# Cross-attention and gated FFN on one core: the sums of a group of heads are added up behind the values of the next group's fourth step instead of its third

## The reference, cut to what matters

```
x = x + xattn(layernorm(x), ctx_2048, mask, ...)     # B=2, N=512, C=512, 1024 context rows, 16 heads of 32
x = x + ffn(layernorm(x), ...)                       # hidden size 1408, weights int - 128, scaled

xattn:  q = w8a8_linear(x, wq, bq)                   # rows quantised to -127..127
        k = cond @ wk.T + bk ;  v = cond @ wv.T + bv
        attn = softmax(q k / sqrt(32) + mask)
        return w8a8_linear(attn v, wo, bo)
ffn:    down(silu(gate(x)) * up(x))
```

## Time and profile before

| | us |
|---|---|
| median of 3 runs | 514.65 |
| lowest, highest | 513.08, 515.75 |
| the profiled execution | 512.79 |
| its span | 511.0 |

### The profile page before, as it was taken

How to read it: one execution, slowest core, us unless ns; L and a number is a source line. 1 busy time by engine, 2 the same in 40 slices (tenths; PEclk the granted TensorE clock), 3 DMA queues, 4 the chain that set the end, 5 groups by cost and what they waited for, 6 DMA issues and landing times.

```text
span 511.0 us, 6924 instructions
## 1 busy us (share of the span) xinstructions
PE 470.5 (92%) x2377; PEld 305.8 (60%) x2377; DVE 365.5 (72%) x482; ACT 262.1 (51%) x465; POOL 243.8 (48%) x134
## 2 busy tenths in 40 slices
PE   4999987799798999999999999998979999899996
PEld 3788765577544455454545454433358878788885
DVE  2889756588758878787878978779876468455235
ACT  3678765322166577575756597467624312322220
POOL 3003300901276879788787869796422212223220
PEclk9999997999989999999999999999989999999999
DMA  7898998993288907346180900030034333336412
GB/s 244 284 339 336 356 290 267 247 352 128 83 183 255 209 18 151 77 95 133 50 178 2 207 21 2 1 124 2 1 124 144 125 123 124 123 124 236 156 62 82
DMA packets 44388, 77.40 MB, mean 151 GB/s; under 512 B 5280, under 2 KB 13504, under 8 KB 44352
## 3 DMA queue, kind: packets, MB, share of 16 engines
q1 hardware_dynamic: 44352, 76.94, 51.2%
HBM read 57.95 MB, written 18.87 MB: 150 GB/s over the span
## 4 chain that ended last, share of the span: by engine, by line
PE 61%; DVE 15%; DMA 5%; issue 4%; ACT 2%; SPq 1%; POOL 1%; ACTq 0%; DVEq 0%; POOLq 0%
PE ps L811 8%; PE ps L781 8%; PE ps L833 8%; PE ps L918 8%; PE ps L919 8%; DVE neg_m L1369 5%; DVE p_sum L1518 5%; PE ps L942 4%; PE ps L941 4%; DMA q_lo_d<-kq_lo 3%; PE ps L730 3%; DMA q_st<-q_hi_d 2%; PE ps L741 2%; PE ps L655 2%; PE ps L656 2%
## 5 line engine op out<-in xcount | busy, mean ns | idle before, releaser
L1369 DVE TENSOR_REDUCE neg_m<-ps 128x1 f32<-128x1024 f32 x128 | 150.1, 1217 | 36.2 <-PE ps L781 36.1
L1119 ACT ACTIVATE p_t<-ps 128x512 f32<-128x512 f32 x256 | 137.2, 598 | 47.7 <-PE ps L811 40.6
L1693 POOL TENSOR_TENSOR p_sum<-p_sum,p_t 128x1024 f32<-128x1024 f32 x46 | 109.6, 2394 | 3.2 <-ACT p_t L1119 0.8
L811 PE MATMUL ps<-q_st,k_st 97*128 97x512 f32 x256 | 97.7, 429 | 5.8 <-ACT p_t L1119 5.7
L1693 POOL TENSOR_TENSOR p_sum<-p_t 128x1024 f32<-128x1024 f32 x30 | 72.0, 2404 | 49.9 <-ACT p_t L1119 39.6
L781 PE MATMUL ps<-k_st,q_st 96*128 96x512 f32 x256 | 82.6, 404 | 5.1 <-DVE mask_sb L1467 1.7
L811 PEld LDWEIGHTS ps<-q_st,k_st 97*128 97x128 f32 x256 | 47.7, 189 | 58.1 <-ACT p_t L1119 36.8
L918 PE MATMUL ps<-xt_hi,k_st 128*128 128x512 f32 x176 | 70.6, 401 | 1.4 <-DVE xt_lo L1475 1.4
L919 PE MATMUL ps<-xt_lo,k_st 128*128 128x512 f32 x176 | 69.7, 396 | 0.0
L1641 POOL TENSOR_TENSOR v_st<-v_st,bv_bc 128x512 f32<-128x512 f32 x16 | 20.1, 1281 | 102.7 <-DVE qin L1314 33.9
L833 PE MATMUL ps<-p_t,v_gr 128*32 128x512 f32 x512 | 68.9, 611 | 0.0
(11 more groups left out here) (138 smaller groups left out, 662.1 us busy)
## 6 DMA issues: line engine op xcount, KB each, us to landing
k_st<-k_hi_d SPq DMA_DIRECT2D x16, 512.0 KB, 6.7
mask_sb<-in_mask SPq DMA_DIRECT2D x3, 2048.0 KB, 10.2
w_int<-in_w_gate SPq DMA_DIRECT2D x22, 256.0 KB, 2.8
w_int<-in_w_up SPq DMA_DIRECT2D x22, 256.0 KB, 3.0
w_int<-in_w_down SPq DMA_DIRECT2D x22, 256.0 KB, 3.6
raw<-in_ctx_t SPq DMA_DIRECT2D x16, 256.0 KB, 5.4
k_hi_d<-kq_hi SPq DMA_DIRECT2D x16, 256.0 KB, 4.0
k_lo_d<-kq_lo SPq DMA_DIRECT2D x16, 256.0 KB, 4.6
```

What stands on the lines that cost most here:

```text
L811: mm = pe.matmul(ps[:, bank, :], k_st[g % SLOTS][0:rows, j, P * lc:P * lc + P], q_st[g % SLOTS][0:rows, j, :], start=True, stop=not with_mask)
L1119: act.activation(p_t[:, q % 4, j, :], ps[:, score_bank(lc, j), :], ACT.Exp).then_inc(exp_done, 1)
L1369: dve.tensor_reduce(neg_m[:, g % 2, nt, j:j + 1], ps[:, bank:bank + 2, :], AX_XY, ALU.max, negate=True).then_inc(max_read, 1)
L1693: pool.tensor_tensor(total, former, p_t[:, q % 4, hs, :], ALU.add).then_inc(added_pool, 1)
```

## The change

One constant, `SUM_LC`, from 2 to 3:

```diff
         SET = 4
-        SUM_LC = 2
+        SUM_LC = 3
         TURN_LC = 4
         HOLD = 1
```

## The result

Over 15 runs of each, the kernel before took 513.58 us (median; 512.42 to 516.38) and the changed one 516.00 us (514.88 to 518.75). The ratio is 1.0052, with a 95% interval from 1.0034 to 1.0071: 1.7 to 3.6 us slower, 2.7 us in the middle. The forecast of +0.8 us (515.4) had the sign, and the time lies in its range, but the step was some three times as large. That 515.4 is only 0.6 us from the measured time is partly luck: the median of three runs that it was added to, 514.65, was itself 1.1 us above the median of the 15.

What follows compares the result with a forecast made beforehand. TensorE made up 61% of the chain, and U waited five times, 4.1 us, for VectorE's reads of a maximum. Terms -1.0 + 0.2 + 1.1 + 0.5 = +0.8 us on the median 514.65 gave 515.4 us, range 512.8 to 517.3.

Steps and rivals of the forecast that it cites:

- Part A: Groups 1 to 4: U's wait goes to M12 and is made good in part, 0.24 us gained four times, -1.0 us.
- The upper end, 0.43 a group: Groups 1 to 4: the gain in each group if M13 does not wait for VectorE.
- Part B: Group 5: ScalarE takes the gain, its exponentials of lc = 4 come later; +0.2 us, between -0.24 and +0.5.
- Part C: Group 6: U, now ahead of O2, waits 0.33, and M14 behind O2 waits for it; +1.1 us, ends 0.6 and 1.3.
- the sign named for it: Profile after, group 6: M14 idle for about 1 us until L1467.
- Part D: Group 7: GpSimd's sum delays VectorE's add and N0's reads, so T waits for VectorE; +0.5 us, between 0 and +1.
- One of the signs named beforehand: Profile after, group 7: T released by L1475.
- The small gain: C and D do not come as worked out and A is at its upper end; -1.1 us, 513.5 us; chance 0.20.
- The whole wait: U's 4.1 us of waits all go, M behind the slot being covered; 510.5 us; chance 0.07.
- The double loss to GpSimd in group 7: GpSimd's sum gets ahead of VectorE's last L1282, another 2.4 us before T; +3.2 us, 517.8 us; chance 0.13.
- The slower side: Whole kernel slower than the range: the slower GpSimd case and the forecast's upper edge; chance 0.14.

Runs made afterwards that it cites:

- group 7 alone: Kernel before with SUM_LC 3 in group 7 only, 2 in the other groups; ratio 1.0049 to the kernel before, median 515.93 us.
- the add put ahead: Changed kernel with VectorE's add of group 7's second quad between the second and third normalised row block instead of in step lc = 3; ratio 1.0015 to kernel before.
- the kernel with U behind O2: Changed kernel with U behind O2 instead of ahead of it in TensorE's queue, in group 6 only; ratio 1.0029 to the kernel before.
- again: The changed kernel, unchanged, in a second series with its own profile; ratio 1.0052 to the kernel before.
- group 6 alone: Kernel before with SUM_LC 3 in group 6 only, 2 in the other groups; ratio 1.0044 to the kernel before, median 514.95 us.
- Groups 1 to 4 alone: Kernel before with SUM_LC 3 in groups 1 to 4 only, 2 in groups 5 to 7; ratios 0.9988 and, in a second series, 0.9974.
- the kernel with O0 later: Kernel before with SUM_LC 3 in groups 1 to 4 and 6, and in group 6 U behind O2 and O0 in step lc = 2; ratios 0.9979 and 0.9964.

## Why the prediction was right or wrong

**Part A held.** Forecast -1.0 us, measured -0.68 to -0.76 over groups 1 to 4. The wait moved to M12 and in a smaller part to M13, U had none. The term was a little too large: M13 started 1.14 behind the release and not 1.11, the pair behind its wait cost 0.57 to the next start and not 0.54, and so the step began at the release + 4.75 and not + 4.68. (The upper end, 0.43 a group, comes to 0.41 by the prediction's own terms.)

**Part B held.** Forecast +0.2 us, measured +0.22 to +0.27. ScalarE's copy of U is what the rest of its step queues behind, and the 0.2 us that TensorE gained does not show.

**Part C held.** Forecast +1.1 us, measured +1.13 and +1.14 in the two profiles where the clock was steady. Both waits of the reckoning were there. U's was 0.28 (forecast 0.33). M14's was 0.43; the sign named for it was about 1 us, which is how much later M14 was to start and not how long it would stand: O2 itself comes later, and the prediction's own terms leave some 0.6 for the wait.

**Part D: the mechanism began as worked out and was priced at the wrong consumer.** Up to the add's end the forecast was right: GpSimd's sum follows at once, the add takes 3.4 us (forecast 354.83 to 358.2; in the kernel with group 7 alone 354.62 to 358.01). The step that failed is "N0's reads follow and end at 359.5, so T starts at 359.6". I followed VectorE's own queue and T's new ring wait, and did not ask who waits for `added_dve`. The exponentials of (7, 4) do: `exps` waits for `added[q - 4, j // 2]`, and `added` of the first quad of a set is the add of the second, which VectorE does in group 7 in the step lc = 3. The add that used to end 0.99 us before those exponentials (356.04 against 357.03) ended behind them, ScalarE held four of them, TensorE held everything behind the fourth score. 1.3 us instead of 0.5, and outside the 0 to +1 given for the part. Group 7 alone shows it, and the add put ahead takes it away. One of the signs named beforehand points at this step: T was to be released by L1475, and it starts right behind the values instead, with those reads over for 0.97 us.

**The clock was missing from the sum.** In steady clock the parts are -0.73 + 0.25 + 1.14 + 1.29 = +1.95 us, a ratio of 1.0038 that lies within the measured 1.0034 to 1.0071. What is above it in the profiles is the lower clock behind the longest waits of TensorE: in group 7, against group 7 alone, D and the stretch behind it together are 0.8 (the kernel with U behind O2), 1.1 (after) and 1.6 us (again) longer; in group 6 1.3 to 1.6 us in the profiles that have it. A single profile of a kernel tells nothing on how often an execution has them, and the clock also fell elsewhere (378.1 to 385.0 in the first profile of the kernel before).

The timed runs can be asked instead: for all series but the first, the mean granted clock of every run of both kernels compared is on record. An estimate from 232 of these runs, those far off left out (a straight line with one slope for all, and a level of its own for each kernel and each series), gives 3.2 us (± 0.3) for 0.01 of the clock. At equal clock, the changed kernel is then 2.1 us (± 0.7) above the kernel before, group 6 alone 1.1 (± 0.8) and group 7 alone 1.9 (± 0.8), against 1.95, 1.14 and 1.29 by the parts. So the parts account for the change at equal clock, within these intervals. (Groups 1 to 4 alone are 0.2 us (± 0.5) faster by the same estimate, less than the 0.7 of the profiles, and the kernel with O0 later 1.2 (± 0.5).) Whether the change also brings the clock down is not shown: its second series ran at 0.979 where the kernel before ran at 0.983, but so did, at the same time, a series of the very kernel before (0.979).

**The rivals.** The small gain did not come, since C was there in full. The whole wait did not go: M12 waited for the same read that U had waited for. The double loss to GpSimd in group 7 did not come either: VectorE's last L1282 got in first and the add was the one that waited. The slower side had too little chance (0.14): both terms behind it, a third consumer and the clock, point one way.

The rule of the Trainium skill ("SBUF — State Buffer", "Who interferes with whom") that the loser of the port pair stands still until the other instruction is over agrees with the trace once more: in group 7 of the changed kernel GpSimd's second sum ends at 354.71 + 4.89 = 359.60 and the add at 360.69, 1.09 behind it, the same distance as the 1.08 in the earlier trace rows.

## What to carry to other kernels

When a piece of work moves out of the way, ask what becomes ready earlier, and whose path that crosses: here GpSimd's sum could have started 1.7 us sooner, started some 0.75 us sooner, and pushed an add of VectorE by 2.2 us that had a slack of 1 us. Follow a delayed instruction through every semaphore it signals, the buffers it frees among them, not only through its own queue. And a wait that is ended by a slower engine's backlog moves to the next in line: moving U saved 0.18 us a group of a wait of some 0.8.

## What the runs showed of the hardware

TensorE's granted clock fell to its lower level for some 3.5 us right behind waits of 1.6 to 1.9 us in otherwise busy stretches, and not each time: behind the 1.64 us wait of group 6 in 5 of 7 profiles with groups 1 to 4 moved and 0 of 4 without, behind the 1.9 us wait of group 7 in 3 of 4, beside the 1.84 us wait at the last T in 5 of 14 (once for 6.9 us). One and the same kernel had it in one profile and not in the next. A fall cost 1.3 to 1.6 us in group 6, about as much as the wait in front of it, 0.8 to 1.6 us in group 7, and 0.6 to 0.9 us at the last T (1.7 for the one of 6.9 us). Over the timed runs, 0.01 of the mean clock goes with 3.2 us (an estimate from the runs of this case).

VectorE's add of 128x1024 in fp32 took 1.2 us by itself, 2.5 us in group 3 and 3.4 us in group 7 of the changed kernel, where GpSimd's sum ran on from the one before. In the last two it ended 1.08 and 1.09 us behind the end of GpSimd's sum.
